# A two-layer scan kernel on one core: the DMAs that spread rows of B for GpSimd are begun by ScalarE

## The chip, the cores and the metric

The kernel runs on one core of one Trainium2 chip. The metric is the device time of one execution in microseconds (us); lower is better. The median of the runs before is 2207.63 us.

## What is computed

x is [8, 96, 32, 32]. Two Mamba layers follow each other. The first runs along the rows of the image (256 sequences of 32 positions, then a layer norm over channels); the second norms again and runs forwards and backwards over the 1024 positions of each image, and the two results are added. Cut to what matters, one layer is:

```
xz = u @ W_in                       # 96 -> 2 x 192
x  = silu(causal_conv4(xr) + conv_b)
dt, B, C = split(x @ W_x)           # 6, 16, 16 columns
delta = softplus(dt @ W_dt + b_dt)
for t:                              # per channel d (192) and state n (16)
    h = exp(delta[t,d] * A[d,n]) * h + delta[t,d] * x[t,d] * B[t,n]
    y[t,d] = sum_n h[d,n] * C[t,n]
out = ((y + x * D) * silu(z)) @ W_out
```

## The kernel before

**Tiling.** Images are taken in pairs. The 2 x 192 channels of a pair fill three tiles of 128 partitions by 1024 positions: channels 0 to 127 of each image, and a mixed tile with the last 64 of both. An item is one direction of one pair (ROWS, FWD or BWD); there are 12 items, and an item has 48 steps: 3 tiles x 16 states. Each step g, 576 in all, is one scan over 1024 positions on VectorE (line 820), which writes `ring[g % 6]`.

**One step.** A scan has two operands, the decay exp(delta * A) and the input u * B, with u = delta * x. Row n of B has to stand on all 128 partitions. It gets there in one of two ways:

- On 424 steps TensorE copies it with a selection matrix into PSUM (`b_ps`, line 485), VectorE multiplies u into it (line 786), and ScalarE writes the decay to `a_ring` (line 623).
- On 152 steps (`BY_POOL`: 11 in a ROWS item, 13 in a FWD item, 14 in a BWD item) a DMA spreads the row from DRAM (`b_rows`) into `b_ring`, which has two slots; GpSimd multiplies u into it (line 877), and ScalarE writes the decay to `b_ps`.

After each scan GpSimd multiplies `ring` by the row of C that another DMA has spread into `c_ring` (four slots; line 883), and TensorE adds the products up in `y_ps` with an identity matrix (line 493), four steps after the scan.

**Order.** Nothing is scheduled automatically: each engine walks the same list of items and steps (`walk`, lines 362 to 384) and does its phases in a fixed order. A phase with a lead does the work of step s + lead. ScalarE has `ahead_a2` (decay to PSUM, lead 1), `ahead_a` (decay to `a_ring`, lead 2), then the jobs of the step. GpSimd has `ahead_b` (the multiply of line 877, lead 3), `product` (line 883), jobs. The sync queue (SP) has `ahead_b` (the row of B, lead 6), `ahead_c` (the row of C, lead 3), jobs. Every queue is in order, and a wait on a semaphore holds what stands behind it. Before the first step of a run of items, each phase is done for as many steps as its lead.

- `look_ahead_b` (lines 449 to 459) issues a row of B once the scan that read the slot's last row is done (`h_ready`); a row for the mixed tile is two DMAs.
- `look_ahead_c` (lines 440 to 447) issues a row of C once the product that read the slot is done (`g_ready`).

**Jobs.** They are what is left of the layers: the preparation of an item that comes (convolution, silu, the small projection that gives dt, B and C, softplus, u) and the end of one that is past (gating, W_out, layer norm), put at chosen steps by the tables `PREP`, `POST` and others. For a FWD item: `xr` at steps 1 to 11 (ScalarE lines 660 and 661, both from a PSUM bank that TensorE filled), `w_out` at 12, 13, 15 and 17 (lines 690 and 691 or 693), `dbl`, the small projection, in halves at 13 and 16. Each half of `dbl` is cut into three bf16 parts: hi on ScalarE (lines 673 and 674), the rest on VectorE (857), mid on ScalarE (681), lo on VectorE (861); the bank is free for TensorE's next product only after lo. Job `bc_in` (SP, step 20) then copies B and C to DRAM and the parts into `dt_in` and `b_in`: 13 DMAs. TensorE's `dt` jobs (line 516) from step 22 wait for `dt_in`.

## Time and profile before

| | |
|---|---|
| median of 3 runs | 2207.63 us (2203.9 to 2212.5) |
| profiled execution | 2207.7 us, its span 2205.9 us |
| VectorE busy | 1956.4 us, 89% |
| GpSimd busy | 1877.5 us, 85% |
| TensorE busy | 1843.4 us, 84% |
| ScalarE busy | 1137.4 us, 52% |
| DMA rings busy | 58.9% of 16 engines' span, 397.20 MB on one queue |
| mean granted TensorE clock | 0.931 |

The share of an engine is over the whole span. Issuing a DMA, waiting for a semaphore and branches are not counted as busy. The scans alone are 968.1 + 344.7 us of VectorE, GpSimd's products of line 883 1353.2 us and its multiplies of line 877 305.5 + 57.0 us. "SPq" is the sync engine's queue; the duration of a DMA there is that of its issue. In a row of the timeline "x2" means that two instructions are merged, and "[1.14 <-DMA ...]" is the idle time before and what ended it. "issue" as a releaser means that the profile shows nothing that was waited for.

### The profile page before, as it was taken

How to read it: one execution, taken by the hardware profiler on the slowest of the kernel's cores; microseconds unless marked ns; L12 is line 12 of the kernel's file. 1: busy time of each engine (PE TensorE's matmuls, PEld its weight loads, DVE VectorE, ACT ScalarE, POOL GpSimd, SP SyncE). 2: the span in 40 equal slices, each digit the busy share in tenths (PEclk: the TensorE clock that was granted, in tenths of full speed). 3: DMA queues.
4: the chain of work that ended last, by engine and by line, in shares of the span. 5: the costliest groups of instructions: out<-in, count | busy, mean ns of one | idle time of the engine just before them, and what ended most of it. 6: DMA issues, size and time to landing. Idle time of an engine off the chain costs nothing. (4 is left out here: it accounts for less than half of the span.)

```text
span 2205.9 us, 16278 instructions
## 1 busy us (share of the span) xinstructions
PE 1843.4 (84%) x4490; PEld 707.5 (32%) x4490; DVE 1956.4 (89%) x1276; ACT 1137.4 (52%) x1256; POOL 1877.5 (85%) x820
## 2 busy tenths in 40 slices
PE   5697889798898899789789779869878888877877
PEld 2232233333333333233333333223323333222322
DVE  2998998879899998998799898999889899799995
ACT  2757464546546436534655644734574563453331
POOL 0887998879898997898889897889889889898995
PEclk9799999999999899999899899999999889989897
DMA  3556556546565755655655675564655675565673
GB/s 82 207 176 164 177 183 169 169 136 226 140 208 196 192 188 180 176 178 196 192 168 191 201 198 166 195 181 167 214 154 182 198 204 168 201 208 174 219 218 82
DMA packets 119591, 398.24 MB, mean 181 GB/s; under 512 B 17788, under 2 KB 22156, under 8 KB 119500
## 3 DMA queue, kind: packets, MB, share of 16 engines
q1 hardware_dynamic: 119500, 397.20, 58.9%
q8 instruction: 36, 0.59, 0.1%
q14 instruction: 55, 0.45, 0.1%
HBM read 386.70 MB, written 6.29 MB: 178 GB/s over the span
## 5 line engine op out<-in xcount | busy, mean ns | idle before, releaser
L883 POOL TENSOR_TENSOR ring<-ring,c_ring 128x1024 f32<-128x1024 f32 x576 | 1353.2, 2369 | 192.7 <-DVE ring L820 191.7
L493 PE MATMUL y_ps<-ring,wp 128*128 128x512 f32 x2304 | 1201.9, 635 | 54.0 <-DVE yv_rows L800 31.2
L820 DVE TENSOR_TENSOR_SCAN ring<-a_ring,b_ps 128x1024 f32<-128x1024 f32 x424 | 968.1, 2283 | 30.3 <-ACT a_ring L623 2.3
L493 PEld LDWEIGHTS y_ps<-ring,wp 128*128 128x128 f32 x2304 | 458.1, 203 | 534.6 <-issue 422.7
L786 DVE TENSOR_TENSOR b_ps<-u_ab,b_ps 128x1024 f32<-128x1024 f32 x256 | 310.4, 1213 | 83.6 <-PE b_ps L485 76.5
L623 ACT ACTIVATE a_ring<-delta_ab,neg_a 128x1024 f32<-128x1024 f32 x256 | 290.7, 1142 | 176.5 <-DVE ring L820 176.1
L820 DVE TENSOR_TENSOR_SCAN ring<-b_ps,b_ring 128x1024 f32<-128x1024 f32 x152 | 344.7, 2274 | 23.1 <-ACT b_ps L623 13.5
L877 POOL TENSOR_TENSOR b_ring<-u_ab,b_ring 128x1024 f32<-128x1024 f32 x128 | 305.5, 2386 | 60.8 <-DMA b_ring<-b_rows 60.7
L623 ACT ACTIVATE a_ring<-delta_m,neg_a 128x1024 f32<-128x1024 f32 x168 | 192.0, 1144 | 255.1 <-DVE ring L820 255.0
L485 PE MATMUL b_ps<-b_in,sel 96*128 96x512 bf16 x512 | 165.6, 407 | 90.0 <-DVE ring L820 89.2
L786 DVE TENSOR_TENSOR b_ps<-u_m,b_ps 128x1024 f32<-128x1024 f32 x168 | 203.0, 1208 | 26.7 <-PE b_ps L485 26.7
L485 PE MATMUL b_ps<-b_in,sel_m 96*128 96x512 bf16 x336 | 111.6, 416 | 117.3 <-DVE ring L820 117.1
L540 PE MATMUL bank<-x,w_conv 96*128 96x512 f32 (+12 forms) x576 | 203.8, 596 | 5.4 <-DVE xs L836 4.9
L623 ACT ACTIVATE b_ps<-delta_ab,neg_a 128x1024 f32<-128x1024 f32 x128 | 142.3, 1114 | 77.9 <-DVE ring L820 77.5
L616 ACT ACT_TABLE_LOAD x116 | 148.8, 1283 | 62.8 <-PE bank L516 38.3
L660 ACT ACTIVATE xs<-bank,wp 128x512 f32<-128x512 f32 x72 | 49.4, 687 | 187.3 <-PE bank L540 187.2
L485 PEld LDWEIGHTS b_ps<-b_in,sel 96*128 96x128 bf16 x512 | 46.3, 103 | 270.7 <-DVE ring L820 137.7
L540 PEld LDWEIGHTS bank<-x,w_conv 96*128 96x128 f32 (+1 forms) x576 | 71.9, 162 | 124.0 <-issue 113.7
L485 PEld LDWEIGHTS b_ps<-b_in,sel_m 96*128 96x128 bf16 x336 | 26.2, 103 | 248.4 <-DVE ring L820 205.2
L516 PE MATMUL bank<-xs,wp 128*96 128x512 f32 x144 | 70.7, 630 | 14.7 <-DVE parts L861 14.7
L836 DVE SCALAR_TENSOR_TENSOR xs<-bank,xs 128x512 f32<-128x512 f32 x72 | 49.1, 682 | 37.9 <-ACT bank L661 37.9
L540 PE MATMUL bank<-io,w_conv 96*128 96x512 f32 (+5 forms) x192 | 66.9, 594 | 13.1 <-DMA io<-x 13.0
(83 smaller groups left out, 1064.0 us busy)
## 6 DMA issues: line engine op xcount, KB each, us to landing
c_ring<-c_rows SPq DMA_DIRECT2D x384, 512.0 KB, 4.8
c_ring<-c_rows SPq DMA_DIRECT2D x384, 256.0 KB, 4.1
b_ring<-b_rows SPq DMA_DIRECT2D x128, 512.0 KB, 4.7
b_ring<-b_rows SPq DMA_DIRECT2D x48, 256.0 KB, 5.2
out<-io SPq DMA_DIRECT2D x16, 192.0 KB, 2.3
io<-x SPq DMA_DIRECT2D x6, 384.0 KB, 4.7
b_in<-parts SPq DMA_DIRECT2D x36, 64.0 KB, 2.0
dt_in<-parts SPq DMA_DIRECT2D x72, 24.0 KB
```

The costliest lines, as they stand in the source:

```text
L485: last = nc.tensor.matmul(half(b_ps[:, g % 2, :], j), pick(k, n), half(b_in[:, parity(kind, pair), :], j), start=True, stop=True)
L493: nc.tensor.matmul(half(y_ps[:, :], j), ident, half(ring[:, g % RING, :], j), start=(n == 0), stop=(n == NS - 1)).then_inc(g_summed, 1)
L516: last = nc.tensor.matmul(bank[0:rows, unit % 2, :], w, m, start=(n == 0), stop=(n == len(terms) - 1))
L540: last = nc.tensor.matmul(o, w, m, start=(d == 0), stop=(d == TAPS - 1))
L616: nc.scalar.preload_act_table_set(name)
L623: nc.scalar.activation(dst, delta_of(kind, pair, k), ACT.Exp, scale=neg_a[:, LAYER[kind], m_of(k) * NS + n:m_of(k) * NS + n + 1]).then_inc ...
L660: nc.scalar.activation(half(xs[:, k, :], j), src, ACT.Identity, bias=bias)
L786: nc.vector.tensor_tensor(b, u_of(kind, pair, k), b, ALU.mult).then_inc(b_used, 1)
L820: nc.vector.tensor_tensor_scan(out=h, data0=a, data1=b, initial=0.0, op0=ALU.mult, op1=ALU.add).then_inc(h_ready, 1)
L836: nc.vector.scalar_tensor_tensor(out=v, in0=bank[:, u % 2, :], scalar=1.0, in1=v, op0=ALU.add, op1=ALU.mult).then_inc(evacuated[u % 2], 1)
L877: nc.gpsimd.tensor_tensor(b, u_of(kind, pair, k), b, ALU.mult).then_inc(b_made, 1)
L883: nc.gpsimd.tensor_tensor(r, r, c_ring[:, g % C_RING, :], ALU.mult).then_inc(g_ready, 1)
```

## The change

SP no longer issues rows of B. `look_ahead_b` goes, and so does its lead on SP; ScalarE gets a phase `rows`, first in its order. A table `rows_begin` says at which step s ScalarE issues the row of step g: the latest of g - 6, the step after the scan that frees the slot, and two steps before the item's own begin. At that step ScalarE waits for `c_kept` (the item's B and C are in DRAM) and for the freed slot, and issues one or two DMAs. Since `rows` has no lead, nothing of it is done before the first step. `spread_row` takes the engine as an argument.

```diff
--- before.py
+++ after.py
@@ -69,12 +69,11 @@
 
 
 PE_ORDER = ("ahead", "sum_0", "jobs", "sum_1")
-ACT_ORDER = ("ahead_a2", "ahead_a", "jobs")
-SP_ORDER = ("ahead_b", "ahead_c", "jobs")
+ACT_ORDER = ("rows", "ahead_a2", "ahead_a", "jobs")
+SP_ORDER = ("ahead_c", "jobs")
 POOL_ORDER = ("ahead_b", "product", "jobs")
 DVE_ORDER = ("take_0", "scan", "take_1", "ahead", "jobs", "last")
 LEAD = {"ahead": 1, "ahead_c": C_LEAD, "ahead_a": 2, "ahead_a2": 1, "ahead_b": 3}
-SP_LEAD = dict(LEAD, ahead_b=B_LEAD)
 SUM_LAG = 4
 
 
@@ -321,6 +320,11 @@
             spread[m % B_RING] += dmas(g)
             b_uses[g] = 16 * spread[m % B_RING]
         b_slot = lambda g: pool_before[g] % B_RING
+        rows_begin = {}
+        for m, g in enumerate(pool_steps):
+            first = g // STEPS * STEPS - 2 if g >= STEPS else 0
+            free = pool_steps[m - B_RING] + 1 if m >= B_RING else 0
+            rows_begin.setdefault(max(g - B_LEAD, first, free, 0), []).append(g)
         a_slot = lambda g: dve_before[g] % A_RING
 
         use_of = {j[:4]: j[5] for p in PARTS for slot in p["slots"] for j in slot}
@@ -384,6 +388,14 @@
                             phases[phase](g0 + s)
 
 
+        def spread_row(eng, dst, rows, k, n, landed_in):
+            if k < 2:
+                eng.dma_start(dst, rows[k, n:n + 1, :].to_broadcast([P, T])).then_inc(landed_in, 16)
+                return
+            for b in range(2):
+                eng.dma_start(dst[b * DM:(b + 1) * DM, :],
+                              rows[b, n:n + 1, :].to_broadcast([DM, T])).then_inc(landed_in, 16)
+
         @block.sync
         def _(sp):
             taps = lambda layer: wpack[0:C, _cols["taps", layer][0]:_cols["taps", layer][0] + TAPS * DI]
@@ -429,14 +441,6 @@
                     landed(sp, name, kind, pair, i)
                     sp.dma_start(half(out[2 * pair + b], j), half(io[:, b, :], j)).then_inc(out_stored, 16)
 
-            def spread_row(dst, rows, k, n, landed_in):
-                if k < 2:
-                    sp.dma_start(dst, rows[k, n:n + 1, :].to_broadcast([P, T])).then_inc(landed_in, 16)
-                    return
-                for b in range(2):
-                    sp.dma_start(dst[b * DM:(b + 1) * DM, :],
-                                 rows[b, n:n + 1, :].to_broadcast([DM, T])).then_inc(landed_in, 16)
-
             def look_ahead_c(g):
                 if g >= ALL_STEPS:
                     return
@@ -444,21 +448,9 @@
                 if g % STEPS == 0:
                     sp.wait_ge(c_kept, 64 * (g // STEPS + 1))
                 wait(sp, g_ready, g - C_RING + 1)
-                spread_row(c_ring[:, g % C_RING, :], c_rows[parity(kind, pair)], k, n, c_spread[g % C_RING])
-
-            def look_ahead_b(g):
-                if g >= ALL_STEPS:
-                    return
-                kind, pair, k, n = step_at(g)
-                if g % STEPS == 0:
-                    sp.wait_ge(c_kept, 64 * (g // STEPS + 1))
-                if by_pool[g]:
-                    m = pool_before[g]
-                    if m >= B_RING:
-                        sp.wait_ge(h_ready, pool_steps[m - B_RING] + 1)
-                    spread_row(b_ring[:, b_slot(g), :], b_rows[parity(kind, pair)], k, n, b_spread[b_slot(g)])
-
-            walk(SP_ORDER, job, SP_LEAD, ahead_b=look_ahead_b, ahead_c=look_ahead_c)
+                spread_row(sp, c_ring[:, g % C_RING, :], c_rows[parity(kind, pair)], k, n, c_spread[g % C_RING])
+
+            walk(SP_ORDER, job, ahead_c=look_ahead_c)
             sp.wait_ge(out_stored, 64 * PAIRS)
 
 
@@ -637,6 +629,15 @@
                 wait(act, h_ready, g - 1)
                 decay(g, b_ps[:, g % 2, :], a_in_psum)
 
+            def rows_at(s):
+                for g in rows_begin.get(s, ()):
+                    kind, pair, k, n = step_at(g)
+                    act.wait_ge(c_kept, 64 * (g // STEPS + 1))
+                    m = pool_before[g]
+                    if m >= B_RING:
+                        act.wait_ge(h_ready, pool_steps[m - B_RING] + 1)
+                    spread_row(nc.scalar, b_ring[:, b_slot(g), :], b_rows[parity(kind, pair)], k, n, b_spread[b_slot(g)])
+
             def full(unit):
                 act.wait_ge(produced[unit % 2], unit // 2 + 1)
                 return bank[:, unit % 2, :]
@@ -714,7 +715,7 @@
                     nc.scalar.activation(x1[:, i, :], x1[:, i, :], ACT.Identity, scale=ln[0:C, 2:3],
                                          bias=ln[0:C, 3:4]).then_inc(affine_done, 1)
 
-            walk(ACT_ORDER, job, ahead_a=look_ahead, ahead_a2=look_ahead_psum)
+            walk(ACT_ORDER, job, ahead_a=look_ahead, ahead_a2=look_ahead_psum, rows=rows_at)
 
 
         @block.vector
```

What this does to the queues, word for word as the built programs stand. First ScalarE in a FWD item, between its steps 13 and 17: `x_out` and `parts` are the two halves' hi and mid parts, `x` and `scratch` the outputs of W_out, `a_ring` and `b_ps` the decays. Before:

```order
L673 ACTIVATE x_out<-bank 96x512
L674 ACTIVATE parts<-bank 44x512
L623 ACTIVATE b_ps<-delta_ab,neg_a 128x1024 x2
L690 ACTIVATE x<-bank 96x512
L691 ACTIVATE scratch<-bank 96x512
L681 ACTIVATE parts<-bank 44x512
L623 ACTIVATE b_ps<-delta_ab,neg_a 128x1024
L623 ACTIVATE a_ring<-delta_ab,neg_a 128x1024
L673 ACTIVATE x_out<-bank 96x512
L674 ACTIVATE parts<-bank 44x512
```

And with the change, the same stretch:

```order
L674 ACTIVATE x_out<-bank 96x512
L675 ACTIVATE parts<-bank 44x512
L393 DMA b_ring<-b_rows 128x1024
L615 ACTIVATE b_ps<-delta_ab,neg_a 128x1024 x2
L691 ACTIVATE x<-bank 96x512
L692 ACTIVATE scratch<-bank 96x512
L682 ACTIVATE parts<-bank 44x512
L393 DMA b_ring<-b_rows 128x1024
L615 ACTIVATE b_ps<-delta_ab,neg_a 128x1024
L615 ACTIVATE a_ring<-delta_ab,neg_a 128x1024
L674 ACTIVATE x_out<-bank 96x512
L675 ACTIVATE parts<-bank 44x512
```

The two DMAs are the rows of steps 16 and 17; that of step 20 follows the last row shown. Each stands behind the jobs of the step before its own.

Second the sync queue at step 20 of the second FWD item, around the copies of `bc_in` (`b_rows` to `b_in`; `io` is a load for a later pair). Before:

```order
L434 DMA b_ring<-b_rows 128x1024
L434 DMA c_ring<-c_rows 128x1024 x2
L414 DMA b_rows<-x_out 32x512
L416 DMA c_rows<-x_out 32x512
L414 DMA b_rows<-x_out 32x512
L416 DMA c_rows<-x_out 32x512
L422 DMA dt_in<-parts 12x2x512 x6
L425 DMA b_in<-parts 32x2x512 x3
L408 DMA io<-x 96x1024 x2
L434 DMA b_ring<-b_rows 128x1024
L434 DMA c_ring<-c_rows 128x1024 x4
```

And with the change:

```order
L393 DMA c_ring<-c_rows 128x1024 x24
L426 DMA b_rows<-x_out 32x512
L428 DMA c_rows<-x_out 32x512
L426 DMA b_rows<-x_out 32x512
L428 DMA c_rows<-x_out 32x512
L434 DMA dt_in<-parts 12x2x512 x6
L437 DMA b_in<-parts 32x2x512 x3
L420 DMA io<-x 96x1024 x2
L393 DMA c_ring<-c_rows 128x1024 x8
```

The rows of B are gone from between the rows of C; the row that stood right behind the load was that of step 27.

## Rows read from the trace of the kernel before

The second FWD item, from 960 to 1147 us of the span, is called item F1; its first step is step 240 of 576.

**Rows 1.** Waits of GpSimd, whole span: engine, tile, releaser; us, times, longest.
```profile
POOL b_ring L877 <- DMA b_ring<-b_rows: 60.7, 22, 6.1
POOL ring L883 <- DMA c_ring<-c_rows: 0.2, 1, 0.2
```

**Rows 2.** Waits of VectorE, whole span.
```profile
DVE b_ps L786 <- PE b_ps L485: 103.3, 69, 6.0
DVE ring L820 <- ACT b_ps L623: 13.5, 30, 1.6
```

**Rows 3.** Timeline, sync queue, item F1: start, us, engine, line, operation, tiles.
```profile
1010.58 0.32 SPq L434 DMA_DIRECT2D b_ring<-b_rows  x1
```

**Rows 4.** Timeline, GpSimd, item F1, steps 16 and 20; idle before and releaser behind.
```profile
1014.76 2.35 POOL L877 TENSOR_TENSOR b_ring<-u_ab,b_ring 128x1024 f32<-128x1024 f32 x1 [1.14 <-DMA b_ring<-b_rows]
1034.78 2.41 POOL L877 TENSOR_TENSOR b_ring<-u_ab,b_ring 128x1024 f32<-128x1024 f32 x1
```

**Rows 5.** The tile b_ring: durations min/median/max of its issues; time to landing.
```profile
L437 SPq DMA_DIRECT2D b_ring<-b_rows x48: 450/596/602, 167.8 to 2142.8; - x48
DMA to landing us min/median/max: 3.5/4.8/9.6
```

**Rows 6.** Timeline, item F1, step 27's row of B, and b_ps of step 24.
```profile
1054.57 0.43 SPq L434 DMA_DIRECT2D b_ring<-b_rows  x1
1061.35 2.37 POOL L877 TENSOR_TENSOR b_ring<-u_ab,b_ring 128x1024 f32<-128x1024 f32 x1 [5.68 <-DMA b_ring<-b_rows]
1055.94 1.23 DVE L786 TENSOR_TENSOR b_ps<-u_ab,b_ps 128x1024 f32<-128x1024 f32 x1 [3.03 <-PE b_ps L485]
```

**Rows 7.** Timeline, ScalarE, item F1, hi parts of steps 13 and 16.
```profile
1017.22 0.58 ACT L674 ACTIVATE parts<-bank 44x512 bf16<-44x512 f32 x1
1029.73 0.58 ACT L674 ACTIVATE parts<-bank 44x512 bf16<-44x512 f32 x1
```

**Rows 8.** Timeline, VectorE, item F1: scans 15 and 16, scan 17, b_ps 18.
```profile
1018.83 4.47 DVE L820 TENSOR_TENSOR_SCAN ring<-b_ps,b_ring 128x1024 f32<-128x1024 f32 x2
1027.99 2.29 DVE L820 TENSOR_TENSOR_SCAN ring<-b_ps,b_ring 128x1024 f32<-128x1024 f32 x1 [1.72 <-issue]
1030.60 1.23 DVE L786 TENSOR_TENSOR b_ps<-u_ab,b_ps 128x1024 f32<-128x1024 f32 x1 [0.32 <-PE b_ps L485]
```

**Rows 9.** Timeline, TensorE, small projection's second half, item F1 and third FWD item.
```profile
1026.42 2.79 PE L516 MATMUL bank<-xs,wp 128*96 128x512 f32 x6 [2.50 <-DVE parts L861]
1558.17 4.47 PE L516 MATMUL bank<-xs,wp 128*96 128x512 f32 x6 [2.50 <-DVE parts L861]
```

**Rows 10.** Windows: us, busy PE, PEld, DVE, ACT, POOL, granted clock, DMA share, GB/s.
```profile
1558.20:1561.50 3.30, 3.30 (x4) 1.18 (x5) 1.78 (x1) 0.00 (x0) 3.30 (x2) 0.50 1.03 359
```

**Rows 11.** Timeline, third FWD item: ScalarE's hi part of step 16, GpSimd's step 20.
```profile
1563.17 0.58 ACT L674 ACTIVATE parts<-bank 44x512 bf16<-44x512 f32 x1
1566.51 2.38 POOL L877 TENSOR_TENSOR b_ring<-u_ab,b_ring 128x1024 f32<-128x1024 f32 x1
```

**Rows 12.** Timeline, last FWD item: b_ps of step 24 on TensorE, then VectorE.
```profile
1941.76 0.59 PE L485 MATMUL b_ps<-b_in,sel 96*128 96x512 bf16 x2
1943.08 1.21 DVE L786 TENSOR_TENSOR b_ps<-u_ab,b_ps 128x1024 f32<-128x1024 f32 x1
```

**Rows 13.** Timeline, item F1: VectorE at step 35; scan 31; GpSimd's products 30 and 31.
```profile
1096.92 1.23 DVE L786 TENSOR_TENSOR b_ps<-u_m,b_ps 128x1024 f32<-128x1024 f32 x1 [5.34 <-PE b_ps L485]
1078.82 2.26 DVE L820 TENSOR_TENSOR_SCAN ring<-b_ps,b_ring 128x1024 f32<-128x1024 f32 x1
1079.84 4.68 POOL L883 TENSOR_TENSOR ring<-ring,c_ring 128x1024 f32<-128x1024 f32 x2
```

**Rows 14.** Timeline, second BWD item, step 15: ScalarE's mid part.
```profile
1202.25 0.58 ACT L681 ACTIVATE parts<-bank 44x512 bf16<-44x512 f32 x1
```

**Rows 15.** Timeline, start: ScalarE's decays of steps 0 and 1; scan 2.
```profile
58.90 2.19 ACT L623 ACTIVATE a_ring<-delta_ab,neg_a 128x1024 f32<-128x1024 f32 x2
65.80 2.26 DVE L820 TENSOR_TENSOR_SCAN ring<-b_ps,b_ring 128x1024 f32<-128x1024 f32 x1
```

## Prediction

> **What bounds the kernel now.** I read the table of engines first: VectorE is busy 89% of the span and GpSimd 85%, so no single engine is full, and the time is set by how these two hold each other up. Then the waits. GpSimd waits 60.7 us for rows of B to land, in 22 waits, and 0.2 us for rows of C [rows 1]. VectorE's largest wait is 103.3 us for TensorE's copies of B into PSUM, and it waits 13.5 us for ScalarE's decays of GpSimd's steps [rows 2]. So only the late rows of B are a DMA matter, and they cost what they make VectorE wait later.
>
> Of those 22 waits I looked at each in the timeline. Fifteen have one pattern, in the FWD items at steps 13, 15, 16 and 17 and in the BWD items at 11 and 19: the sync queue issues the row within 0.03 us of the scan that frees the slot, and GpSimd waits for the transfer. The freed slot is the limit there, not the queue. For step 16 of the second FWD item (960 to 1147 us, "item F1" from here) the issue is at 1010.58 [rows 3] and GpSimd begins the multiply at 1014.76, 4.18 us later, after a wait of 1.14 [rows 4]; landing takes 3.5 to 9.6 us, median 4.8, and a row for the mixed tile takes two issues of 0.6 [rows 5]. The other seven waits (20.3 us together) are all of step 27, whose row comes behind the thirteen copies of a preparation (and, in F1, a load) on the sync queue: in F1 it is issued at 1054.57 and GpSimd stands 5.68 us for it [rows 6].
>
> **What moves.** 128 issues of 0.32 us (one row to 128 partitions) and 48 issues for the mixed tile go from SP to ScalarE, each with its wait for the freed slot. On SP nothing but C, loads, stores and preparation copies remains. Wherever SP's wait for a slot held back rows of C, GpSimd did not need them yet: 0.2 us in all [rows 1]. Freeing C is worth nothing.
>
> On ScalarE a row of step g now stands at step max(g-6, freed+1), behind all jobs of the step before. ScalarE is an in-order queue whose jobs wait for TensorE, so the question is when it gets there. I compared, for all 152 rows, the start of the instruction that will stand ahead of the issue with SP's present issue time.
>
> 1. **FWD items, step 16.** Its slot is freed by scan 13, so the issue stands behind the jobs of step 13, whose last is the hi part of the small projection, begun at 1017.22 in F1 [rows 7]. The queue can issue at 1017.27 against 1010.58 now: 6.7 us later. GpSimd begins at 1017.27 + 4.18 = 1021.45 and ends 2.35 later, 1023.8. Scan 16, the second of two that end at 1023.30, started at 1021.04 [rows 8]: it becomes 2.8 us late. I read 2.7, 2.8, 2.7 and 1.9 in the four FWD items. Behind that scan VectorE has the lo part of the projection, TensorE waits for it (2.50 idle before its six matmuls [rows 9]), and then come b_ps of step 18, for which VectorE already waits 0.32 [rows 8], and ScalarE's second hi part. So the 2.8 us go round the whole loop.
>
> 2. **The clock.** TensorE idles 2.50 us before those six matmuls. In F1 they take 2.79 us, in the next FWD item 4.47 [rows 9], where the granted clock reads 0.50, the 1.2 GHz level, after that same idle stretch [rows 10]. With 2.7 us more idle I take the lower level in all four items, where now two have it: 1.7 us more in F0 and F1. The Trainium skill ("TensorE: Matmul & The Clock Gate", What's actually happening) says that the default is throttled and activity releases it; the rows at 0.50 agree. By it alone one would expect this lengthening to cost clock, as I do.
>
> 3. **FWD items, step 20.** Its row stands behind the second hi part: 1029.73 in F1 [rows 7], plus 2.8, plus 4.2 to GpSimd's start = 1036.7 against 1034.78 [rows 4]: 1.9 late, or 3.6 with the slow matmuls. In the third FWD item 1563.17 + 2.7 + 4.2 = 1570.1 against 1566.51 [rows 11]: 3.6. In the last likewise 3.5. From there GpSimd runs without a gap to the product of step 19, which releases the last C slot ahead of the preparation's copies on SP; these end in TensorE's dt matmul, and VectorE waits for it at step 24 (3.03 in F1 [rows 6]). So GpSimd's lateness, not VectorE's, is what leaves step 24: 3.6 + 3.6 + 3.6, and 2.8 in the last item, where b_ps of step 24 is done at 1942.35 and wanted at 1943.08, 0.7 us of slack [rows 12]. Sum **+13.6**; with the fast clock in F0 and F1 it would be 10.2.
>
> 4. **Step 27.** ScalarE reaches it some 10 us before SP did, and GpSimd's 5.44 to 0.27 us vanish in FWD. But VectorE feels that only at step 35, where it waits 5.34 us behind GpSimd's norm and u jobs [rows 13], and by step 31 GpSimd had nearly caught up: its product there began about 1.0 us after scan 31, which ended at 1081.08 [rows 13]. Gain 0.9 + 1.0 + 0.1 + 0 = **-2.0**. In BWD the product of step 24 waits for its scan anyway: 0.
>
> 5. **BWD items, step 19.** SP issues it as scan 15 ends; ScalarE comes to it behind the mid part, which in the second BWD item begins at 1202.25 [rows 14], 0.4 us after SP's issue: 0.4 us late to GpSimd, then by the same chain to step 24, three times: **+1.1**. Steps 11 and 16 become 2 to 4 us late too, but each scan still starts 2 us or more after its product would be ready.
>
> 6. **Start.** The first row (step 2) was issued before any work; now it follows ScalarE's first two decays, the second begun at 59.96 [rows 15]. 60.0 + 4.8 + 2.35 = 67.1 against scan 2 at 65.80 [rows 15]: **+1.3** (0.1 with the fastest landing, 2.4 if it goes out at that decay's end).
>
> 7. **ScalarE's own time.** 128 issues of 0.32 and 24 pairs of 0.6 are 70 us on a half-idle engine. I followed each into the next decays: none that a scan waited for moves by more than its slack. 0; the upper bound is 0.35 us at each of the 30 waits of VectorE for a decay [rows 2], 10 us. No row shows a DMA issued by ScalarE. If it goes out only when the ACTIVATE ahead ends, 0.5 us are added at three places of each FWD item, some 4 us in all.
>
> The Trainium skill ("DMA: Bandwidth & Descriptors", Issuing engines are not separate DMA queues) says that issuing from several engines saves only the sequencer's time. By it the gain could be no more than SP's 70 us of issuing, none of it on a path here, so the page speaks against a gain; the 0.32 us of [rows 3] agree.
>
> **The sum.** 13.6 - 2.0 + 1.1 + 1.3 = +14.0 on the profiled execution's 2207.7 us (span 2205.9), which is the median of the runs, 2207.63, within 0.1. That is 2221.7; since item 2 may fail in one place, I give **2221**.
>
> **Rivals.** *Hidden* (same): ScalarE's lateness in FWD is mostly absorbed, the clock stays up, landings on a queue of their own are as quick as 3.5 us instead of 4.2. Each FWD site then gives 1 to 1.5, and the sum is 4 to 6, less 2, plus 0 to 2.4 for items 5 and 6: 2210 to 2214. For it: the waits of step 16 differ by 3 us between items as it is. *Freed queue* (faster): SP's waits for slots did hold the preparation copies, so that dt and step 24 come earlier. VectorE's idle at step 24 is 20.4 us over six items (3.03 in F1 [rows 6]) and 1.7 us at step 17 of each FWD item [rows 8]: 27 us at most, 2180. It would decide if the preparation copies began earlier than now; against it, what stands ahead of them is C of step 23, which waits for GpSimd's product of step 19, and GpSimd has no gap there. *Dear issue* (slower still): each issue holds ScalarE for 1 us or more, decays become late at the 30 places and the bounds of 7 are all paid: 14 + 10 + 4 = +28, 2236, or more.
>
> **Chances.** Forecast 0.45, hidden 0.33, freed queue 0.07, dear issue 0.15. A measurement here tells 0.5%, 11 us, from no change. Over 2218.7: most of the forecast's cases and all of the last, 0.58. Faster than 2196.6: 0.07. Within: 0.35. The range goes from 2206, where only the gain of item 4 is felt, to 2238, just over the last case's 2236.
>
> **What would show it.** In F1's counterpart: step 16's row issued right after the hi part, GpSimd idle there some 5 us instead of 1.1 and scan 16 waiting for it, less than 1 us of the wait at step 17 left, TensorE's six matmuls near 4.5 us. GpSimd's whole wait for b_ring stays near 60 us, but moves: the 20 us at step 27 go, about 7 come at the start, the rest at steps 11 to 20. Waits for C stay near 0. Wrong if step 16 does not wait longer, if step 27 still waits, or if VectorE's wait for ScalarE grows by more than 5 us.

## The result, and the profile after

The changed kernel takes **2238.9 us** (median of 4 runs, 2237.2 to 2242.6) beside 2210.1 for the kernel before (4 runs, 2203.9 to 2213.2): a ratio of 1.0140, 95% interval 1.0124 to 1.0155, or 27 to 34 us. The profiled execution took 2237.2 us with a span of 2235.2, at a mean granted clock of 0.933 (before 0.931). The direction was forecast, the size only to a half: +14 was forecast, +29 came, and the median is 0.9 us above the top of the range.

The costliest groups of the page, from its part 5 (line, engine, operation, tiles, shapes, count | busy us, mean ns | idle before, releaser):

```profile
L878 POOL TENSOR_TENSOR b_ring<-u_ab,b_ring 128x1024 f32<-128x1024 f32 x128 | 306.1, 2391 | 78.0 <-DMA b_ring<-b_rows 77.9
L508 PE MATMUL bank<-xs,wp 128*96 128x512 f32 x144 | 76.2, 672 | 39.6 <-DVE parts L862 39.6
```

The second line stood in the page of before as

```profile
L516 PE MATMUL bank<-xs,wp 128*96 128x512 f32 x144 | 70.7, 630 | 14.7 <-DVE parts L861 14.7
```

These are the matmuls of the small projection. TensorE stands 24.9 us longer idle ahead of them, behind VectorE's lo parts, and they are busy 5.5 us longer: 30.4 us, about as much as was lost. (Idle time of one engine need not be lost time of the kernel; the experiments have to show that it is.) GpSimd's wait for rows of B grew by 17.2 us [rows 1]. The waits of the changed kernel (engine, tile, releaser; us, times, longest):

```profile
POOL b_ring L878 <- DMA b_ring<-b_rows: 77.9, 24, 6.8
POOL ring L884 <- DMA c_ring<-c_rows: 8.3, 3, 3.3
DVE b_ps L787 <- PE b_ps L477: 115.9, 70, 6.7
DVE ring L821 <- ACT b_ps L615: 13.3, 30, 1.6
DVE ring L821 <- POOL b_ring L878: 10.3, 5, 3.0
```

VectorE waits 12.6 us longer for b_ps and no longer for ScalarE's decays than before [rows 2]. So ScalarE's decays are no later than they were. The landings are as they were too (the tile b_ring; the issue of a mixed row took 0.60 on SP and takes 0.56 here [rows 5]):

```profile
L393 ACTq DMA_DIRECT2D b_ring<-b_rows x128: 320/326/358, 58.2 to 2132.2; - x128
L396 ACTq DMA_DIRECT2D b_ring<-b_rows x48: 451/558/735, 167.7 to 2171.2; - x48
DMA to landing us min/median/max: 3.3/4.8/10.3
```

**Where it comes.** Start of a scan after, less its start before, from the two timelines ("enters" is the item's first scan; the items are called F0 to F3):

| us | enters the item | scan 16 | scan 20 | leaves | the item costs |
|---|---|---|---|---|---|
| FWD 0 | 0.5 | 2.9 | 7.5 | 5.1 | 4.6 |
| FWD 1 (F1) | 6.0 | 7.4 | 14.2 | 12.2 | 6.2 |
| FWD 2 | 12.1 | 14.8 | 20.0 | 20.1 | 8.1 |
| FWD 3 | 19.9 | 21.9 | 25.3 | 29.2 | 9.3 |

The four FWD items carry 28.1 of the 29.3 us at the last scan. Of these 20.0 come between scan 16 and scan 20, where the forecast had some 4, of which 3.4 were the clock in two items. What happens there, in F1's counterpart (timeline: start, us, engine, line, operation, count, idle before and releaser):

```profile
1021.09 0.33 ACTq L393 DMA_DIRECT2D b_ring<-b_rows  x1
1021.52 0.58 ACT L675 ACTIVATE parts<-bank 44x512 bf16<-44x512 f32 x1
...
1025.97 2.35 POOL L878 TENSOR_TENSOR b_ring<-u_ab,b_ring 128x1024 f32<-128x1024 f32 x1 [6.19 <-DMA b_ring<-b_rows]
...
1028.41 2.29 DVE L821 TENSOR_TENSOR_SCAN ring<-b_ps,b_ring 128x1024 f32<-128x1024 f32 x1 [2.99 <-POOL b_ring L878]
...
1030.62 6.67 DVE L852 SCALAR_TENSOR_TENSOR yv_fwd<-xs,wp,yv_fwd 128x1024 f32<-128x1024 f32 x2
1032.89 8.90 POOL L884 TENSOR_TENSOR ring<-ring,c_ring 128x1024 f32<-128x1024 f32 x3
1037.21 0.67 DVE L862 TENSOR_TENSOR parts<-bank,parts 44x512 bf16<-44x512 f32 x1
...
1038.03 5.40 PE L508 MATMUL bank<-xs,wp 128*96 128x512 f32 x6 [9.81 <-DVE parts L862]
...
1043.53 0.33 ACTq L393 DMA_DIRECT2D b_ring<-b_rows  x1
...
1044.83 1.23 DVE L787 TENSOR_TENSOR b_ps<-u_ab,b_ps 128x1024 f32<-128x1024 f32 x1 [4.75 <-PE b_ps L477]
...
1048.19 2.39 POOL L878 TENSOR_TENSOR b_ring<-u_ab,b_ring 128x1024 f32<-128x1024 f32 x1 [6.40 <-DMA b_ring<-b_rows]
```

The first four lines are the prediction's item 1: the row leaves only with the hi part, GpSimd stands 6.19 us instead of 1.14 [rows 4], and scan 16 waits 2.99. Then something comes that I had not seen. Behind scan 16 VectorE has two *skip operations* (the D term, yv += D·xs). Before the change they took, and the second line is the same piece of the timeline of before:

```profile
1023.22 2.45 DVE L851 SCALAR_TENSOR_TENSOR yv_fwd<-xs,wp,yv_fwd 128x1024 f32<-128x1024 f32 x2
...
1026.42 2.79 PE L516 MATMUL bank<-xs,wp 128*96 128x512 f32 x6 [2.50 <-DVE parts L861]
```

They ran almost wholly while GpSimd stood idle for step 17's row (1020.41 to 1025.18). Now GpSimd, late with step 16, finds step 17's row landed and works without a pause, and the same two operations take 6.67 us. The lo part comes 4.2 us later on top of the late scan, TensorE has idled 9.81 us instead of 2.50, and its six matmuls take 5.40 instead of 2.79, at the lower of its two clock levels (the granted clock reads 0.50 from 1038.1 to 1043.3, and 1.00 beside the matmuls of before). From 18.5 us the stretch from scan 16 to scan 20 grows to 25.4. All twelve skip operations of the kernel together, three in each FWD item, take 30.7 us instead of 22.5.

### The profile page after: what moved, and what is told of

The parts are those of the page before. It is cut to its first block and busy times, and to the rows that moved or that the text cites. A ratio compares the mean times of both kernels' runs of the same rounds, so it can differ in the third digit from the quotient of the medians.

```text
span 2235.2 us, 16417 instructions
## 1 busy us (share of the span) xinstructions
PE 1832.6 (82%) x4490; PEld 702.5 (31%) x4490; DVE 1964.3 (88%) x1276; ACT 1137.9 (51%) x1256; POOL 1881.2 (84%) x820
## 5 line engine op out<-in xcount | busy, mean ns | idle before, releaser
L485 PE MATMUL y_ps<-ring,wp 128*128 128x512 f32 x2304 | 1189.9, 630 | 55.2 <-DVE yv_rows L801 29.5
L485 PEld LDWEIGHTS y_ps<-ring,wp 128*128 128x128 f32 x2304 | 452.6, 201 | 530.9 <-issue 419.1
L878 POOL TENSOR_TENSOR b_ring<-u_ab,b_ring 128x1024 f32<-128x1024 f32 x128 | 306.1, 2391 | 78.0 <-DMA b_ring<-b_rows 77.9
L821 DVE TENSOR_TENSOR_SCAN ring<-b_ps,b_ring 128x1024 f32<-128x1024 f32 x152 | 344.9, 2273 | 26.6 <-ACT b_ps L615 13.3
L608 ACT ACT_TABLE_LOAD x116 | 148.8, 1283 | 60.7 <-PE bank L508 37.4
L508 PE MATMUL bank<-xs,wp 128*96 128x512 f32 x144 | 76.2, 672 | 39.6 <-DVE parts L862 39.6
L532 PE MATMUL bank<-io,w_conv 96*128 96x512 f32 (+5 forms) x192 | 66.9, 594 | 13.7 <-DMA io<-x 13.5
```

The costliest lines, as they stand in the source:

```text
L485: nc.tensor.matmul(half(y_ps[:, :], j), ident, half(ring[:, g % RING, :], j), start=(n == 0), stop=(n == NS - 1)).then_inc(g_summed, 1)
L508: last = nc.tensor.matmul(bank[0:rows, unit % 2, :], w, m, start=(n == 0), stop=(n == len(terms) - 1))
L532: last = nc.tensor.matmul(o, w, m, start=(d == 0), stop=(d == TAPS - 1))
L608: nc.scalar.preload_act_table_set(name)
L821: nc.vector.tensor_tensor_scan(out=h, data0=a, data1=b, initial=0.0, op0=ALU.mult, op1=ALU.add).then_inc(h_ready, 1)
L878: nc.gpsimd.tensor_tensor(b, u_of(kind, pair, k), b, ALU.mult).then_inc(b_made, 1)
```

## The experiments

Theory **T**: the place of the row of FWD step 16 behind jobs that wait for TensorE makes scan 16 late; that slides the skip operations under GpSimd's work, and with the clock it makes up most of the loss of the FWD items, 15 to 25 us (12 to 25 for the row alone in the kernel before). Rivals: **R1**, issuing costs ScalarE its time; **R2**, two queues at work make landings slower. "Before" is 2208 to 2210 us in each comparison, the kernel before on the same chip. Where two changed kernels are compared, each is taken less its own before. Runs of one kernel differ by up to 15 us (before, 16 runs: 2200.6 to 2215.2), and a profile shows one run alone.

A function `on_sp(kind, pair, s)` is added to the changed kernel for several of them: rows of B for which it is true go by the sync queue, at the place and with the wait that they had before; the others stay with ScalarE.

**1. Only step 16 of the FWD items back on the sync queue.**

```
on_sp = lambda kind, pair, s: kind == FWD and s == 16
```

> The changed kernel, but the row of step 16 of the four FWD items is issued by the sync queue again; all other rows of B stay with ScalarE. Theory (late row of step 16, carried on): the late row shifts scan 16 by 2 to 3 us, that puts VectorE's two skip operations (6.67 us instead of 2.45 in item F1) under GpSimd's work and leaves TensorE's six matmuls at the lower clock, so that this one row carries most of the 28 us that the FWD items lost. The time falls by 15 to 25 us against the changed kernel, to 2213 to 2224 us; what is left over before is step 20's row and the start. In item F1 scan 16 waits for nothing again and the two skip operations take about 2.5 us. Rival 1 (the issues cost ScalarE its time): 176 issues remain but for 8, so the time stays at 2236 or more. Rival 2 (two queues at work at once make the landings slower): stays near 2236 too, since 144 rows still leave from ScalarE.

Measured: 2218.6 us (2213.0 to 2224.8), ratio to before 1.0048 (1.0031 to 1.0065). It stands 9.6 us over its before where the changed kernel stands 28.8: four rows of 152 give back 19.2 us. In F1 the pair of skip operations is short again, and the matmuls are quick (this profile is of the fastest of the five runs; in all four items the pair is short in it):

```profile
1023.87 2.46 DVE L868 SCALAR_TENSOR_TENSOR yv_fwd<-xs,wp,yv_fwd 128x1024 f32<-128x1024 f32 x2
...
1027.07 2.79 PE L522 MATMUL bank<-xs,wp 128*96 128x512 f32 x6 [2.50 <-DVE parts L878]
```

As T says; R1 and R2 would have left it at 2236 or more.

**2. The other way round: before, and only step 16 of the FWD items on ScalarE.**

```
on_sp = lambda kind, pair, s: not (kind == FWD and s == 16)
```

> The kernel before, but only the row of step 16 of the four FWD items is issued by ScalarE, at the place where the changed kernel issues it. Theory: scan 16 is late by 2 to 3 us in each FWD item, the skip operations and the six matmuls after it take longer, and the time rises by 12 to 25 us over before, to 2222 to 2235. Rival 1 (ScalarE's time) and rival 2 (two queues): 4 rows in 4 items change nothing that is measurable, 2208 to 2212. Rival 3 (the damage of the changed kernel comes at step 20, whatever step 16 does): below 5 us.

Measured: 2224.7 us (2222.3 to 2230.7), ratio 1.0071 (1.0051 to 1.0090), +15.7 us from four rows. F0 alone costs 13.5 us in this profile, which is of the slowest of the four runs, and shows the collision at its worst:

```profile
490.17 2.41 POOL L894 TENSOR_TENSOR b_ring<-u_ab,b_ring 128x1024 f32<-128x1024 f32 x1 [11.08 <-DMA b_ring<-b_rows]
...
494.80 2.43 POOL L894 TENSOR_TENSOR b_ring<-u_ab,b_ring 128x1024 f32<-128x1024 f32 x1
494.87 13.81 DVE L868 SCALAR_TENSOR_TENSOR yv_fwd<-xs,wp,yv_fwd 128x1024 f32<-128x1024 f32 x2
497.10 7.02 POOL L900 TENSOR_TENSOR ring<-ring,c_ring 128x1024 f32<-128x1024 f32 x3
503.98 2.43 POOL L894 TENSOR_TENSOR b_ring<-u_ab,b_ring 128x1024 f32<-128x1024 f32 x1
```

The skip operation begins 0.07 us behind GpSimd's multiply and gets through only when GpSimd stops, five instructions later; GpSimd's own three products take 7.02 us, undisturbed. In F1 to F3 of this profile one of the two takes 3.4 us, and nothing is starved. The durations of the nine on yv_fwd (min/median/max in ns), here, and of before:

```profile
L868 DVE SCALAR_TENSOR_TENSOR yv_fwd<-xs,wp,yv_fwd x9: 1257/1260/12619, 484.0 to 1573.4; 128x1024 f32<-128x1024 f32 x9
```
```profile
L851 DVE SCALAR_TENSOR_TENSOR yv_fwd<-xs,wp,yv_fwd x9: 1256/1279/3364, 482.4 to 1556.2; 128x1024 f32<-128x1024 f32 x9
```

and of the changed kernel, where the median itself is the slow form:

```profile
L852 DVE SCALAR_TENSOR_TENSOR yv_fwd<-xs,wp,yv_fwd x9: 1257/3354/3393, 482.9 to 1573.1; 128x1024 f32<-128x1024 f32 x9
```

The 3364 of before was in the trace that I predicted from: the one at step 14 of F1, which also begins 0.07 us behind a multiply of GpSimd, but gets through behind it and makes the product after it longer (3.34 us). The same distance of 0.07 us thus led to 3.36 us once and to 12.62 once; what decides between them, no run shows. The Trainium skill ("SBUF — State Buffer", Who interferes with whom) says that a VectorE instruction with two SBUF inputs contends with a GpSimd instruction that reads SBUF. The scans here, and the multiplies into b_ps, have an operand in PSUM and do not slow down (scan with b_ring: mean 2274 ns before, 2273 after, at most 2292 in both; the multiplies at most 1230), so the trace agrees.

**3. What issuing costs ScalarE.** The kernel before, with an additional DMA issued by ScalarE at each of the 176 places:

```
+ACT_ORDER = ("tiny", "ahead_a2", "ahead_a", "jobs")
...
+nc.scalar.dma_start(tiny_out[i * C:(i + 1) * C, :], eps[:, :]).then_inc(tiny_done, 16)
```

> The kernel before, and at the same 176 places in ScalarE's order it also issues a DMA of 96 values of 4 bytes that waits for nothing; all rows of B stay with the sync queue. It prices the issuing by itself. Theory: 176 issues of 0.3 to 0.6 us lie in ScalarE's slack, 2207 to 2213 us, within 3 us of before. Rival 1 (issuing costs ScalarE its time, decays come late): 10 us or more over before, with VectorE's wait for ScalarE's decays up from 13.5 us by more than 5.

Measured: 2334.4 us, ratio 1.0572 (1.0551 to 1.0594), where 2207 to 2213 was expected. That looks like R1 and is not. VectorE waits no longer for ScalarE's decays than before (13.5 us [rows 2]), GpSimd waits for rows of C (0.2 [rows 1]):

```profile
POOL ring L899 <- DMA c_ring<-c_rows: 150.1, 69, 6.3
...
DVE ring L836 <- ACT b_ps L630: 13.3, 23, 1.6
```

and in the page's list of DMA issues the 512-KB rows of C take 9.2 us to land instead of 4.8:

```profile
c_ring<-c_rows SPq DMA_DIRECT2D x384, 512.0 KB, 9.2
```

96 packets of 4 bytes for each issue made a bad probe. With one packet (`tiny_out[i:i + 1, :], eps[0:1, :]`):

> The kernel before, and at the same 176 places in ScalarE's order it also issues a DMA of one packet of 4 bytes. The version with 96 packets each was no price of issuing: the packets made the landings of B and C rows twice as long. With one packet the landings should stay at 4.7 us. Theory: the issuing lies in ScalarE's slack, 2207 to 2213. Rival 1 (issuing costs ScalarE its time): 10 us or more over before with landings as before. If SP's own issues become longer beside ScalarE's, up to 4 us.

Measured: 2210.4 us, ratio 0.9996 (0.9984 to 1.0009), with 4.8 and 4.6 us for those two landings and

```profile
DVE ring L836 <- ACT b_ps L630: 14.0, 29, 1.6
```

So 176 issues cost nothing: R1 falls, within 2 us. These issues wait for nothing; the wait for the freed slot, which the rows of B have besides, is in the next experiment.

**4. The same queue, another place.** All 152 rows stay with ScalarE, ahead of the jobs of the step whose scan frees the slot:

```
-ACT_ORDER = ("rows", "ahead_a2", "ahead_a", "jobs")
+ACT_ORDER = ("ahead_a2", "ahead_a", "rows", "jobs")
...
-free = pool_steps[m - B_RING] + 1 if m >= B_RING else 0
-rows_begin.setdefault(max(g - B_LEAD, first, free, 0), []).append(g)
+free = pool_steps[m - B_RING] if m >= B_RING else 0
+rows_begin.setdefault(max(g - B_LEAD - 1, first, free, 0), []).append(g)
```

> All 152 rows of B still issued by ScalarE, but ahead of the jobs of the step whose scan frees the slot, where the changed kernel has them behind these jobs. Same engine, same queue, same number of issues; only the place differs. Theory (the place, behind TensorE-dependent jobs, is what costs): the row of FWD step 16 goes out within 1 us of the scan that frees it, and the time falls to 2208 to 2217. Rivals 1 and 2 (ScalarE's time, or the second queue): stays above 2230. Risk for the theory: ScalarE now waits for a scan ahead of its jobs, which could make these jobs late and leave 5 us or more.

Measured: 2215.2 us (2213.1 to 2218.4), ratio 1.0033 (1.0021 to 1.0044). It stands 5.3 us over its before: 23.6 of the 28.8 us go, with the engine, the queue and the number of issues unchanged, so R1 and R2 fall for that part. Step 16's row in F1 leaves 0.09 us behind the end of scan 13 (the first line) again, and GpSimd stands 1.06 us for it (1.14 before [rows 4]):

```profile
1007.89 2.29 DVE L821 TENSOR_TENSOR_SCAN ring<-b_ps,b_ring 128x1024 f32<-128x1024 f32 x1 [0.34 <-ACT b_ps L615]
...
1010.27 0.35 ACTq L393 DMA_DIRECT2D b_ring<-b_rows  x1
...
1015.99 2.36 POOL L878 TENSOR_TENSOR b_ring<-u_ab,b_ring 128x1024 f32<-128x1024 f32 x1 [1.06 <-DMA b_ring<-b_rows]
```

**5. How much of it is the collision.** The twelve skip operations of the preparations (nine on yv_fwd, three on yv_rows) left out, each replaced by a copy of one column; the D term is missing from these outputs. The expectations speak of nine; the edit takes out all twelve. In the changed kernel and in the one before:

```
-nc.vector.scalar_tensor_tensor(out=y, in0=xs[:, i, :], scalar=sm[:, m_of(i), 6:7], in1=y, op0=ALU.mult, op1=ALU.add)...
+nc.vector.tensor_copy(y[:, 0:1], y[:, 0:1])...
```

> The changed kernel without the nine skip operations of VectorE of the FWD and BWD preparations (each is replaced by a copy of one column, so the D term is left out of these outputs). Theory (the skips collide with GpSimd's work, which makes the late row dear): beside the same removal in the kernel before, the change costs 8 to 18 us instead of 29. Rival (the skips only cost their own busy time): this kernel and the one before without skips differ by the same 29 us.

> The kernel before without the same nine skip operations (the D term left out there). Control of the run before. Theory: TensorE's 2.50 us idle ahead of its six matmuls falls to about 0.1, VectorE has 2.5 us less to do on that path in each of four items, and the time falls by 5 to 12 us, to 2196 to 2203.

Measured: 2220.2 us (ratio to before 1.0048, 1.0032 to 1.0064) and 2205.7 us (0.9983, 0.9971 to 0.9995). Without these operations the change costs 14.5 us (10 to 19 by the two intervals); with them 28.8. The kernel before gained 4 us by the removal, less than the 5 to 12 expected. TensorE's idle time ahead of the small projection grows by 8.7 us where it grew by 24.9 (the changed kernel's page, then that of before, both without skips; these two profiles differ by only 5.2 us, the first being of one of its faster runs, so 8.7 may be low):

```profile
L508 PE MATMUL bank<-xs,wp 128*96 128x512 f32 x144 | 68.1, 611 | 15.2 <-DVE parts L861 15.2
```
```profile
L516 PE MATMUL bank<-xs,wp 128*96 128x512 f32 x144 | 66.4, 598 | 6.5 <-DVE parts L860 6.5
```

**6. The skip operations later**, at steps 14, 21 and 22 instead of 14, 16 and 16 of the FWD items, in both kernels:

```
+BWD_SKIP = (14, 21, 22)
...
-out.append((at["skip"][k], "skip", k))
+out.append((at["skip"][k] if kind != BWD else BWD_SKIP[k], "skip", k))
```

> The changed kernel, but VectorE's skip operations stand at steps 14, 21 and 22 of the FWD items instead of 14, 16 and 16, behind the second round of the small projection instead of ahead of it. All rows of B stay with ScalarE. Theory (the late row matters because VectorE's two skip operations then run beside GpSimd's work and everything behind them waits): without them ahead of the projection the loop from step 16 to 20 is 4 to 9 us shorter in each FWD item, and the time falls by 12 us or more against the changed kernel, to 2226 or less. Rival (the skips only take the time that VectorE must give them anyway, at whatever step): 2235 to 2240.

> The kernel before with the same move of the skip operations to steps 14, 21 and 22. It is the control of the run before: what the move is worth where the rows are early. Theory: there the two operations run in 2.45 us while GpSimd waits for step 17's row, and at steps 21 and 22 they run beside GpSimd's work; the move gains what TensorE waits less for the projection and loses the slower operations: 2203 to 2211. The late row then costs less than the 29 us with the old order: the difference of the two runs is 10 to 20 us. Rival: the difference stays at 29.

Measured: 2221.9 us (1.0067, 1.0051 to 1.0084) with the change, 2217.2 (1.0043, 1.0029 to 1.0056) without. The late rows now cost 4.7 us (about 1 to 10 by the two intervals), less than the 10 to 20 expected. The control missed its expectation of 2203 to 2211: at their new place the operations run beside GpSimd in the kernel before too,

```profile
L852 DVE SCALAR_TENSOR_TENSOR yv_fwd<-xs,wp,yv_fwd x9: 2472/3069/4530, 486.3 to 1591.7; 128x1024 f32<-128x1024 f32 x9
```

and none of the nine has the 1.26 us of its undisturbed form. So part of what closes the gap is that the control got worse.

**7. Only their order changed**: the lo part of step 16 ahead of the two skip operations (the skip loop of the FWD items' list moved behind that of the projection).

> The changed kernel with the same exchange of lo part and skip operations. Theory: what the collision of the skip operations with GpSimd costs is passed on through the lo part, for which TensorE waits 9.8 us in item F1; with the lo part ahead of them the six matmuls begin 6.7 us earlier, and the time falls by 8 to 20 us against the changed kernel, to 2219 to 2231. Rival (the two operations hold up scan 17 as much as they did the lo part): 2235 or more.

> The kernel before, with the skip operations of one step put behind that step's part of the small projection (VectorE's order at step 16 becomes scan 15, scan 16, lo part, skip, skip, where it was scan, scan, skip, skip, lo part). Rows of B by the sync queue. TensorE's six matmuls can begin 2.4 us earlier in the four FWD items; in the run without skip operations that, and 2.5 us less work, gave about 4 us. The two skip operations then begin 0.7 us later, just ahead of GpSimd's multiply for step 17. Theory: 0 to 8 us faster, 2202 to 2210; if the second one collides with that multiply, GpSimd's side loses about 2 us per item and nothing is won. Rival: slower by up to 5.

Measured: 2221.1 us (1.0060, 1.0038 to 1.0081) with the change, 2211.8 (1.0019, 1.0005 to 1.0032) without. The changed kernel stands 13.3 us over before instead of 28.8, and 9.2 over the kernel before with the same exchange: it gains 15.5 us from an exchange that shortens no operation. In F1 (lo part, skips, six matmuls; this profile is of the fastest of six runs):

```profile
1021.91 0.66 DVE L866 TENSOR_TENSOR parts<-bank,parts 44x512 bf16<-44x512 f32 x1
1022.49 6.14 DVE L856 SCALAR_TENSOR_TENSOR yv_fwd<-xs,wp,yv_fwd 128x1024 f32<-128x1024 f32 x2
1022.72 2.79 PE L512 MATMUL bank<-xs,wp 128*96 128x512 f32 x6 [2.86 <-DVE parts L866]
```

The pair is nearly as slow as in the changed kernel, 6.14 us beside 6.67, but TensorE no longer waits behind it, and its matmuls take 2.79 us. So most of what the collision costs goes through the lo part and TensorE. Not all of it: in F3 of this profile a skip operation is starved a second time, for 12.08 us, and scan 17 stands behind the pair:

```profile
1913.05 13.27 DVE L856 SCALAR_TENSOR_TENSOR yv_rows<-xs,wp,yv_rows 128x1024 f32<-128x1024 f32 x2
...
1926.25 2.28 DVE L825 TENSOR_TENSOR_SCAN ring<-b_ps,b_ring 128x1024 f32<-128x1024 f32 x1
```

That scan comes 9.0 us later behind scan 16 than before, and the item keeps 7.4 us, as much as this profile's last scan is late in all. The kernel before does not gain by the exchange, it loses 1 to 7 us, where a gain of up to 8 was expected; the cause stays open.

**8. The other rows.** Steps 11 to 20 of the FWD items on the sync queue (`kind == FWD and 11 <= s <= 20`), all FWD rows there (`kind == FWD`), or all but those of step 27 (`not (kind != ROWS and s == 27)`):

> The changed kernel, but the rows of steps 11 to 20 of the four FWD items (24 rows) are issued by the sync queue again; the other 128 rows stay with ScalarE. The run with only step 16 back on the sync queue recovered about 20 of the 29 us. Theory: the rest of the FWD loss is the rows of steps 13, 15 and 20 behind ScalarE's jobs, so this run comes to 2210 to 2217, and what stays over before is step 27 (the run with step 27 alone on ScalarE was some 4 us slower than before) and the start (1 us). Rival 2 (two queues make the landings slower): 128 rows on ScalarE's queue keep it at 2218 or more.

> The changed kernel, but all rows of the FWD items go by the sync queue as before; ScalarE keeps those of the ROWS and BWD items and the start. It prices my items 5 and 6 alone (BWD step 19, and the first row behind two decays): forecast 1.1 + 1.3 = +2.4 over before, 2208 to 2213. If the BWD items carry the 5 us that stayed when every row left ScalarE early, it comes to 2212 to 2216; if the FWD items carry them, within 2 us of before.

> The kernel before, but only the rows of step 27 of the FWD and BWD items, which came behind the preparation's copies on the sync queue, are issued by ScalarE. Theory: GpSimd's waits at step 27 (20.3 us in seven places) go, and the time falls by the 2 us of my item 4, to 2204 to 2209; at best by 6. Rival (freed queue): the sync queue reaches its loads and C earlier, a gain of more than 8 us. Rival (the row was hidden anyway): 0.

Measured: 2213.8 us (1.0026, 1.0015 to 1.0037), 2212.7 (1.0015, 1.0002 to 1.0027) and 2213.1 (1.0017, 1.0006 to 1.0029). The first shows that 128 rows on ScalarE's queue cost about 6 us (3 to 8) in all, which leaves little for R2. The second prices the rows of BWD and ROWS and the start, items 5 and 6, at 3.7 us over its own before, where I had 2.4. The third is the miss: item 4 promised a gain of 2 and got a loss of 1 to 6. GpSimd's wait for B does fall, from 60.7 [rows 1] to 42.2 us, but part of it comes back as a wait for C (0.2 before [rows 1]):

```profile
L900 POOL TENSOR_TENSOR ring<-ring,c_ring 128x1024 f32<-128x1024 f32 x576 | 1351.8, 2365 | 215.3 <-DVE ring L837 207.1 <-DMA c_ring<-c_rows 7.4
```

C of step 24 and later stands behind the same copies on the sync queue as row 27 did. And the row now leaves beside these copies, 0.4 us ahead of the first in F1 (ScalarE's row, then the first of the sync queue's four copies and the six loads of dt_in):

```profile
1047.84 0.33 ACTq L395 DMA_DIRECT2D b_ring<-b_rows  x1
1048.22 0.38 SPq L428 DMA_DIRECT2D b_rows<-x_out  x1
...
1050.59 5.06 SPq L436 DMA_DIRECT2D dt_in<-parts  x6
```

The four copies take 0.38, 0.42, 0.52 and 0.89 us; before, they took 0.38, 0.42, 0.42 and 0.42, and dt_in began 1.81 us behind the first, here 2.37. dt_in leads to the dt matmul for which VectorE waits at step 24, and scan 24 comes 0.9 to 1.2 us later behind scan 23 than before in all four FWD items; that the 0.6 us are the reason is argued, not shown. What item 4 had promised behind step 24 is there in F0 and F1, 0.8 and 2.4 us; F2 and F3 lose 1.1 and 0.6 there. The profile can't price it better: 3.9 of the 5.0 us by which its last scan is late arose ahead of F0, where the two kernels do the same. So I take from it that no gain is left over, not that the row costs 4 us.

**9. The last 5 us.** To the kernel of experiment 4, with either step 27's rows or the rows of the BWD items back on the sync queue:

> The kernel with all rows on ScalarE ahead of the jobs of the freeing step (2215 us, 5 to 7 over before), but the rows of step 27 of the FWD and BWD items go back to the sync queue behind the preparation's copies. The run with only these rows on ScalarE was some 4 us slower than before: they then leave beside the copies, whose issues on the sync queue become longer (0.3 to 0.9 us in all). Theory: this run comes back to within 3 us of before, 2208 to 2213. Rival (what stays is the second queue or ScalarE's time in general, the step-27 run was scatter): it stays at 2214 to 2217.

> The kernel with all rows on ScalarE ahead of the jobs of the freeing step (2215 us), but the rows of the BWD items go by the sync queue as before. In its profile 6.3 of the 9.2 us that it ends later than before came between steps 23 and 24 of three BWD items, where VectorE waits for the dt matmul. Theory: these go, 2207 to 2212. Rival (the last 5 us are spread, or of the FWD items and step 27): it stays at 2213 to 2217.

Measured: 2214.2 us (1.0033, 1.0017 to 1.0049) and 2208.2 us (0.9992, 0.9981 to 1.0002). Less their own before these are 6.4 and -0.9 us, where the kernel of experiment 4 had 5.3. The first missed its expectation of 2208 to 2213: step 27 changes nothing there. The BWD rows are the whole of it, 6.1 us. In the profile of experiment 4, 6.2 us arise between scans 20 and 24 of three BWD items; which wait of the chain does it was not taken apart. The last kernel issues the 52 rows of the FWD items and the 44 of ROWS from ScalarE, early, and is the equal of before: between 0.4 us slower and 4 us faster. No version here beats the kernel before by more than that.

**The account**, by what each run stands over its own before: 28.8 us in all; 9.6 once step 16 of FWD is back on the sync queue; 5.9 with its neighbours from 11 to 20; 3.7 with all of FWD. So step 16 is 19 us, its neighbours 4, the other FWD rows 2, the rest (BWD, ROWS and the start) 4, each with some 3 to 5 us of uncertainty; the two small ones are not clear of nothing.

## Where the prediction failed, and where it held

**Bottleneck and place: right.** The lost time is in the FWD items, from late rows of B through GpSimd, VectorE and TensorE.

**Item 1: right in size.** 2.7, 2.8, 2.7 and 1.9 us late at scan 16 were forecast; 2.4, 3.1, 2.7 and 2.0 came (scan 16 against scan 15; F1 had made up 1.7 us of its lateness by then). Most of the signs came as well: 6.2 us idle at step 16, where "some 5" stood, nothing left of the wait at step 17, none at step 27, matmuls at 5.4 where 4.5 stood, VectorE's wait for ScalarE unchanged. One did not: GpSimd's whole wait for rows of B was to stay near 60 us and is 77.9.

**The step that failed** is the sentence behind it: "Behind that scan VectorE has the lo part of the projection", "so the 2.8 us go round the whole loop". Between the two stand the skip operations. The prediction does not name them, and so its sum leaves them at the 2.45 us of before. They are the only operations of that stretch with both inputs in SBUF, and their 2.45 held only because GpSimd was waiting for a row just then. The late row took that wait away: +4.2 us in F1, and 14.3 us of the total by the runs without them (10 to 19). Without these operations the change costs 14.5 us; the forecast sum was 14.0. That the two are so close is partly luck: the measured one is known to some 4 us, and items 4 and 6 of the sum did not come as written.

**Item 2: right in sign, small in size.** The six matmuls took 4.9 to 5.4 us in all four items, where the lower level had been forecast for all: 2.5, 2.6 and 0.9 us longer in the first three and 0.5 less in the last; the last two had the lower level before, as the prediction says. The group of 144 is busy 5.5 us longer, where 3.4 stood.

**Item 3: undersized.** Step 20's row was forecast 3.6 us late at GpSimd, on top of nothing from the collision; it came 13.4 us later than before in F1, 6.0 of which F1 had inherited. From scan 15 to scan 24 the four items lose 5.5, 9.2, 7.7 and 8.4 us, 30.8 in all, where 13.6 stood. That step 24 passes most of it on was right: the items keep 4.6 to 9.3 us each.

**Item 4: wrong.** -2.0 was forecast. GpSimd's waits for step 27's row went, but in F0 and F1 they moved to C of step 24 behind the same copies, which I had ruled out ("Waits for C stay near 0": they are 8.3 us, 6.1 of them there and 2.2 in the last BWD item). Between scan 24 and the end of the item F0 and F1 do make up 1.0 and 1.3 us, as forecast; F2 and F3 lose 0.4 and 0.9. Taken alone, with what it brings ahead of step 24, it measured +1 to +6.

**Items 5 and 6: together within the noise**, 2.4 forecast, 3.7 measured (0.4 to 6). Taken singly, item 6 did not come. The first row did not wait for the two decays:

```profile
58.20 0.34 ACTq L393 DMA_DIRECT2D b_ring<-b_rows  x1
59.47 2.19 ACT L615 ACTIVATE a_ring<-delta_ab,neg_a 128x1024 f32<-128x1024 f32 x2
...
63.04 2.39 POOL L878 TENSOR_TENSOR b_ring<-u_ab,b_ring 128x1024 f32<-128x1024 f32 x1 [4.89 <-DMA b_ring<-b_rows]
...
66.37 2.27 DVE L821 TENSOR_TENSOR_SCAN ring<-b_ps,b_ring 128x1024 f32<-128x1024 f32 x1
```

GpSimd is done at 65.43, and scan 2 starts 0.56 us later than before, as scans 0 and 1 do: nothing is lost there, where 1.3 stood. The first three BWD items cost 1.5, -0.5 and -0.2 us in this profile, against 1.1 for the three.

**Item 7: right.** Zero, with an interval of -3.5 to +2 us. The rival "dear issue" named 2236, nearer the result than my number, by a mechanism that the runs exclude.

**Range.** It ended just over the dear-issue rival because no case had the late row make the work behind it longer. A bound was at hand: the skips at their slow form in every item, 2 times 2.1 us, four times, is 17 us, on top of 14.

## What to carry to other kernels

When a delay is moved along a chain, the durations on it are not constants: for each VectorE operation with both inputs in SBUF ask what GpSimd does beside it now, and what it will do then. The min/median/max of its tile (1256/1279/3364 ns) shows at a glance that it has two prices. A DMA issue cost the issuing engine nothing measurable here (176 of them, -3.5 to +2 us), but its place can delay the transfer by all that the jobs ahead of it wait: the same 152 rows cost 28.8 us behind the jobs and 5.3 ahead of them. What another engine waits for (the lo part) may go ahead of what can be starved; here that paid with late rows, by 15.5 us, and cost 1 to 7 in the kernel before.

## What the hardware showed that I had not expected

- A VectorE operation with two SBUF inputs, begun 0.07 us behind a GpSimd one, was held for five back-to-back GpSimd instructions, 12.6 us instead of 1.26; the GpSimd ones were not slowed. It happened twice in the profiles shown (experiments 2 and 7; the second began 0.61 us behind the GpSimd instruction and took 12.08 us, again for five). Where it came between them it cost 3.36 us, and the products beside a pair of skips took 8.90 us for three instead of 7.0.
- ScalarE's queue issues a DMA before the ACTIVATEs ahead of it have run: in F1 step 16's row left at 1021.09, ahead of the hi part's ACTIVATE at 1021.52, behind which it stands in program order; the first row left 1.27 us ahead of the decays. So neither item 7's 0.5 us for each row nor item 6's 1.3 us were there.
- 176 DMAs of 96 packets of 4 bytes, 68 KB in all, made the 512-KB rows of C land in 9.2 us instead of 4.8 and the kernel 126 us slower; 176 of one packet changed nothing measurable (0.9984 to 1.0009).
